# An attention step rebuilt: products with the values in one burst, scores beside transposed scores, projections at the step's end

## The reference

```python
# layer 0: 16 heads of 8, rotary positions, no mask
Q, K, V = rope(ln(x) @ Wq.T), rope(ctx @ Wk.T), ctx @ Wv.T
x = x + softmax(Q K^T / sqrt(8)) V @ Wo.T
x = x + relu(ln(x) @ quant(W1).T + b1) @ quant(W2).T + b2
# layer 1: 16 query heads on 4 key/value heads, causal and given mask, LayerNorm on the attention's output
q, k, v = ln(x) @ Wq.T + bq, ctx @ Wk.T + bk, ctx @ Wv.T + bv
x = x + ln(softmax(where(mask, q k^T / sqrt(8), min)) v) @ Wo.T + bo
# a mixture of 8 experts, one for each token
x = x + score * expert_of(ln(x))
```

## Time and profile before

| | |
|---|---|
| median of 3 runs | 578.75 us (578.5 to 578.78) |
| the profiled execution: its own time, which is its span | 578.6 us |
| tensor engine, matmuls | 493.0 us, 85% |
| vector engine | 399.0 us, 69% |
| scalar engine | 357.1 us, 62% |
| GpSimd | 372.8 us, 64% |

### The profile page before, as it was taken

The page is one execution under the profiler, slowest core; times in us unless marked ns, Lnnn a source line. Parts: engine busy times, 40 slices in busy tenths (PEclk is TensorE's granted clock), DMA queues, the critical chain, the costliest instruction groups (busy, mean ns, idle before and its releaser), DMA issues.

```text
span 578.6 us, 20130 instructions
## 1 busy us (share of the span) xinstructions
PE 493.0 (85%) x6238; PEld 361.9 (63%) x6239; DVE 399.0 (69%) x1248; ACT 357.1 (62%) x872; POOL 372.8 (64%) x755
## 2 busy tenths in 40 slices
PE   3587899999997799988999999999998834999993
PEld 2455666666665599976455555555554423999992
DVE  6687777777888578645578888888888762444441
ACT  4356677777766555653566776777765643666661
POOL 6868766676772367676556688888885561455552
PEclk9879999999999999999899999999999965999997
DMA  6664353534332860004433545444543114333330
GB/s 170 159 135 110 88 131 81 127 88 114 104 76 56 265 156 1 2 19 126 110 91 94 127 128 143 106 111 130 146 121 93 36 68 134 94 91 98 101 87 27
DMA packets 102161, 59.92 MB, mean 104 GB/s; under 512 B 20338, under 2 KB 98178, under 8 KB 102098
## 3 DMA queue, kind: packets, MB, share of 16 engines
q1 hardware_dynamic: 98738, 51.79, 35.5%
q0 software_dynamic: 2784, 6.82, 3.4%
q10 hardware_dynamic: 576, 0.53, 0.3%
HBM read 19.90 MB, written 8.81 MB: 50 GB/s over the span
## 4 chain that ended last, share of the span: by engine, by line
PE 47%; DVE 14%; issue 13%; SPq 8%; DMA 7%; POOL 5%; ACT 4%; ACTq 1%; DVEq 0%; POOLq 0%
DVE negmax L1448 6%; PE bank L688 6%; PE score L632 4%; PE bank L802 4%; PE scoreT L792 4%; DMA stack<-pieces 3%; PE bank L866 3%; PE bank L575 3%; PE bank L544 3%; SPq L404 3%; PE bank L703 2%; PE scoreT L854 2%; PE scoreT L661 2%; PE score L601 2%; SPq L470 2%
## 5 line engine op out<-in xcount | busy, mean ns | idle before, releaser
L1448 DVE TENSOR_REDUCE negmax<-score 128x8 f32<-128x1024 f32 x128 | 156.2, 1220 | 29.9 <-PE score L632 20.1
L975 ACT ACTIVATE P<-scoreT 128x1024 f32<-128x1024 f32 x128 | 131.0, 1024 | 40.1 <-PE scoreT L652 20.3
L688 PE MATMUL bank<-P,Vc 128*32 128x128 f32 x2048 | 82.7, 279 | 2.3 <-DVE product L1556 1.2
L632 PE MATMUL score<-stack 64*128 64x128 bf16 x1024 | 62.3, 221 | 15.6 <-DVE negmax L1448 9.5
L1337 POOL DMA_INDIRECT out<-by x39 | 40.2, 1031 | 51.3 <-issue 26.8
L632 PEld LDWEIGHTS score<-stack 64*128 64x128 bf16 x1024 | 33.6, 95 | 42.0 <-issue 23.1
L688 PEld LDWEIGHTS bank<-P,Vc 128*32 128x32 f32 x2048 | 48.6, 109 | 16.4 <-issue 4.3
L981 ACT COPY outs<-bank 128x256 f32<-128x256 f32 x64 | 23.7, 370 | 49.2 <-PE bank L688 49.2
L1199 POOL TENSOR_TENSOR pieces<-full,pieces 128x256 bf16<-128x256 f32 x63 | 42.2, 670 | 12.8 <-ACT pieces L956 12.8
L1202 POOL TENSOR_TENSOR pieces<-rest,pieces 128x256 bf16<-128x256 f32 x63 | 43.7, 693 | 4.9
L866 PE MATMUL bank<-M,bhT 128*128 x312 | 43.5, 282 | 0.3 <-ACT bhT L1102 0.3
(11 more groups left out here) (219 smaller groups left out, 1261.7 us busy)
## 6 DMA issues: line engine op xcount, KB each, us to landing
stack<-pieces SPq DMA_DIRECT2D x192, 128.0 KB, 2.5
ctxT<-in_ctxT SPq DMA_DIRECT2D x32, 128.0 KB, 2.4
XB<-expert_rows SPq DMA_DIRECT2D x39, 66.0 KB
XA<-expert_rows SPq DMA_DIRECT2D x39, 64.0 KB
XR<-in_x SPq DMA_DIRECT2D x4, 512.0 KB, 4.3
stack<-blank SPq DMA_DIRECT2D x32, 64.0 KB, 2.1
stack<-negpT SPq DMA_DIRECT2D x64, 32.0 KB, 1.9
M<-in_M SPq DMA_DIRECT2D x1, 2048.0 KB, 9.8
```

What stands on the lines that cost most here:

```text
L632: mm = nc.tensor.matmul(SCORE[:, r, i * 128:(i + 1) * 128], Qs[pb][rows, h, tb * S:(tb + 1) * S], Ks[pb][rows, kv, tb * S:(tb + 1) * S], s ...
L688: mm = nc.tensor.matmul(PVOUT[VCOL * i:VCOL * (i + 1), half * 128:(half + 1) * 128], Vc[:, k % BODY, at:at + VCOL], P32[:, c, i * 128:(i + ...
L975: nc.scalar.activation(P32[:, half * 2:half * 2 + 2, :], SCORET[:], ACT.Exp, scale=SCALE).then_inc(sem("exp_done"), 1)
L1448: nc.vector.tensor_reduce(negmax[:, k % 2, :, half * HQ:(half + 1) * HQ], SCORE[:].rearrange("p r (h k) -> p r h k", h=HQ), AX.X, ALU.max, ...
```

## The change

Its core is a new order of the step on each engine. On the tensor engine:

```diff
                 def step(t, j):
                     scores(t + 2, 0, j + 2)
+                    scoresT(t, 0, j)
+                    pv(t - 1, 0, j - 1)
                     pv(t - 1, 1, j - 1)
-                    scoresT(t, 0, j)
                     max_transpose(t + 1)
                     out_transpose(t - 2)
-                    regroup(t - 1, j - 1)
-                    if L and j % 2 == 0:
-                        base_logits(j + 6)
-                    project(j, 0)
-                    project(j, 1)
+                    if j % 2 == 0:
+                        project_v(j + 4)
+                    else:
+                        xn_transposes(j + 7)
+                    scores(t + 2, 1, j + 2)
                     scoresT(t, 1, j)
-                    scores(t + 2, 1, j + 2)
-                    pv(t, 0, j)
                     out_project(t - 2)
+                    regroup(t - 1)
                     if j % 2 == 0:
-                        project_v(j + 4, t)
+                        project_k(j + 6, 0)
+                        project_k(j + 6, 1)
                     else:
-                        xn_transposes(j + 7, t)
-                    if L and j % 2 == 1:
-                        ranks(j - 5)
+                        if L:
+                            base_logits(j + 7)
+                        project_q(j + 7, 0)
+                        project_q(j + 7, 1)
+                        if L:
+                            ranks(j - 5)
```

Both halves of `P` of one batch now wait for the next step, so `P32` has six half banks in place of four, three halves in turn, and `exps` waits for the product two halves back:

```diff
-                        act.wait_ge(sem("pv_done"), count(2 * (t + T0) + half - 1))
+                        act.wait_ge(sem("pv_done"), count(2 * (t + T0) + half - 2))
```

Vector engine. Layer 0: `maxima`, `rotate`, `maxima`, `denominators`, `norm_out`, `add_out(t - 2)`. Layer 1, where it was one function for both layers:

```diff
+                def step1(t, j):
+                    if j % 2 == 1:
+                        values(j + 3)
+                        if t > B:
+                            score((t - 7) // 2)
+                    else:
+                        place_of((t - 6) // 2)
+                    maxima(t + 2, 0, j + 2)
+                    add_out(t - 3, j - 3)
+                    if j % 2 == 0:
+                        base_values(j + 6)
+                        make_mask(j + 4)
+                        mean_shift((t - 6) // 2)
+                    else:
+                        choose((t - 5) // 2)
+                    maxima(t + 2, 1, j + 2)
+                    denominators(t - 1)
+                    norm_out(t - 1)
+                    out_stats(t - 1, j - 1)
+                    tile_stats(t - 3)
+                    if j % 2 == 1:
+                        carry((t - 5) // 2)
+                        if t < B:
+                            score((t - 7) // 2)
```

Scalar engine and GpSimd:

```diff
                     else:
                         high(j + 5, 0)
-                    evac_outs(t - 1)
-                    exps(t, 0)
-                    evac_max(t + 1, j + 1)
-                    evac_out(t - 2)
-                    exps(t, 1)
...
+                    exps(t, 0, j)
+                    evac_max(t + 1, j + 1)
+                    evac_out(t - 2)
+                    evac_outs(t - 1)
+                    if j % 2 == 1:
+                        evac_xnT(j + 7)
+                    exps(t, 1, j)
...
                         if j % 2 == 0:
-                            out_rstd((t - 2) // 2)
                             add_bias(j + 4)
                         else:
                             mean_rstd((t - 5) // 2)
                         for i in scattered_at(t):
                             scatter(i)
+                        if j % 2 == 0:
+                            out_rstd((t - 2) // 2)
```

More of the change, by code:

```diff
@@ L177, in build @@
         W1e = [sb(f"W1e{i}", [128, FF])[:] for i in range(TURNS)]
-        bhT = [sb(f"bhT{i}", [128, FF])[:] for i in range(TURNS)]
+        bhT = [P32[:, QUARTERS - 1 + i, :] for i in range(TURNS)]
         XA = [sb(f"XA{i}", [128, D])[:] for i in range(TURNS)]
@@ L254, in rows_of, with p_slot @@
             return tile[s:s + 15 * STRIDE + 1:STRIDE]
+        def p_slot(L, k, half):
+            return (2 * (L * B + k % BODY) + half) % SLOTS_OF_P
         def both_pieces(b, s):
@@ L270, in run_early, with body_loop @@
                 run(step, p - (PAIRS - EARLY) - AHEAD)
-        def body_loop(eng, step, first=-AHEAD, before=None, end=B + 3):
+        def body_loop(eng, step, first=-AHEAD, before=None, end=B + 3, nb=NB):
             for t in range(first, BODY):
@@ L278, in body_loop @@
                 run(step, t)
-            with eng.Fori(1, NB) as i:
+            with eng.Fori(1, nb) as i:
                 body["i"] = i
@@ L282, in body_loop @@
                     step(i * BODY + j, j)
-            for t in range(NB * BODY, end):
+            for t in range(nb * BODY, end):
                 if before and t in before:
@@ L679, in pv @@
                         pe.wait_ge(sem("outs_ready"), count(t + T0))
+                        headed_seen(t - 1)
                         pe.wait_ge(sem("v_ready"), (pair(k) + P0) + 1)
-                        if L and k % 2 == 0:
-                            pe.wait_ge(sem("ranks_read"), count(pair(k) - 2))
                     pe.wait_ge(sem("exp_done"), 2 * (t + T0) + half + 1)
@@ L729, in out_project @@
                         pe.wait_ge(sem("outT_ready"), t + T0 + 1)
+                        if isinstance(t, int) and t + 2 in folds:
+                            folds[t + 2]()
                         mm = nc.tensor.matmul(OUTX if L else OUTP, oT[:], WO, start=True, stop=True)
@@ L872, in experts @@
                 block_loop(pe, step, -2, BLOCKS)
-            step = attention(0)
-            for t in range(-AHEAD, START):
-                run(step, t)
             def gate_turn():
@@ L1009, in normalise @@
                         act.wait_ge(sem("xn_transposed"), count(p + P0))
-                        for i in range(2):
+                        for i in tiles:
                             x = X[:, 2 * p + i, :] if isinstance(p, int) else X[:, bass.ds(p * 2 + i, 1), :].rearrange("p o d -> p (o d)")
@@ L1569, in score, with step0 @@
                         nc.vector.reciprocal(XR[:, tiles, SCORE_AT], top[:, 2, tiles]).then_inc(sem("scored"), 1)
-                def step(t, j):
-                    if L and j % 2 == 1:
-                        values(j + 3)
-                        base_values(j + 5)
-                    add_out(t - 3, j - 3)
-                    if L == 0 and isinstance(t, int) and 0 <= t <= 3:
+                def step0(t, j):
+                    if isinstance(t, int) and 0 <= t <= 3:
                         x_group(3 + t)
-                    if L and t > B and j % 2 == 1:
-                        score((t - 7) // 2)
@@ L1608, in attention @@
+                step = (step0, step1)[L]
                 return step
```

127 lines of the change are left out of this document (54 added, 73 removed).

## The result

The changed kernel takes 588.8 us (median; 584.9 to 591.1) against 578.75: 1.5% **slower**, ratio 1.015 with a 95% interval of 1.0097 to 1.0203. A ratio is the recorded one, which is not exactly the quotient of the medians.

The account below looks back on a forecast made before the run. Layer 0 nearly bound by the tensor engine, layer 1 by a ring of waits through tensor, vector and GpSimd engines. 578.6 - 15.7 + 1.5 = 564.4, with 1.6 us for full rings 566 us; range 555 to 575.

Parts of the forecast that it names:

- the sum of 564.4: Whole kernel: profiled span 578.6 us, less 15.7 for layer 0, plus 1.5 for layer 1, before 1.6 us allowance.
- Outside of the attentions I count nothing: FFN and the rest outside both attentions: folds take as long, experts' tile only changes address, so 0 us.
- the ring: Layer 1, waits between maxima's transposes through vector engine and GpSimd: 6.07 plus 6.42 us, 12.5 for two steps against 12.17.
- a switch that the new order of the masks saves: Layer 1, even step's transpose of maxima to second maxima: one matmul-kind switch fewer, making that piece 1.5 us.
- by the vector engine alone: Layer 1, even to odd transpose of maxima: vector engine's work without GpSimd's wait would take 5.8 us.
- The first 7 steps: Layer 1's steps ahead of the 21, without gate work yet: 5.75 us each against about 6.0, so -1.9 us.
- the tensor engine's sum: Layer 0: tensor-engine pieces added in the new order, 4.42 even and 4.19 odd, 8.6 us for two against 10.08.
- two full rings: Layer 0: tensor engine 8.6 and DMA ring 8.6 to 8.7 us, neither without loss, so 8.8 for two steps.
- half the gain: Layer 0's 7 steps before and 8 after the steady 17: 15 x 0.32 = 4.8 us less.
- Both layers gain: Rival, chance 0.18: the transpose of maxima costs layer 1 nothing, layer 1 gains 9 us, whole kernel 554.
- The DMA ring holds layer 0 back: Rival, chance 0.17: late transfers make layer 0 9.4 us for two steps, gain 8 us in all, 572.
- The slower rival: Chance 0.10: GpSimd's even step in layer 1 pushes the split, two steps 13.9 us, 581; decides from 13.7.

Follow-up runs that it names:

- run 2: The changed kernel with layer 0 put back to its old step, only layer 1 new: 598.1 us, 1.026 of the kernel before.
- run 4: The changed kernel with the transposed-score matmuls of layer 0's last eight steps issued twice: 591.3 us, 1.016 of the kernel before.
- run 3: The changed kernel with add_out ahead of the first maxima again in layer 1's even steps: 581.2 us, 0.998 of the kernel before.
- run 5: run 3's kernel with GpSimd's out_rstd moved behind split_max of layer 1's odd step: 580.8 us, 0.992 of the kernel before.
- run 6: The changed kernel with SP's six transfers of a pair in layer 0 issued as two and four: 581.6 us, 0.997 of the kernel before.
- run 8: The changed kernel with the edits of run 3, run 5 and run 6 together: 576.8 us, 0.986 of the kernel before.
- run 9: The changed kernel with base_values of layer 1's early steps ahead of the FFN's additions: 587.5 us, 1.012 of the kernel before.

## Why the prediction was wrong

It said 566 us, faster with a chance of 0.86; the kernel is slower, at 588.8. Against the profiled span the sum of 564.4 was 18.7 us short: 4.1 in layer 0, 6.6 in layer 1, 8.8 in the FFN's part, 0.8 too much behind it.

**The step that failed is "Outside of the attentions I count nothing"**: 0 forecast, +8.8 measured. The change also gave a new order to the early steps of layer 1 that run between the FFN's tiles. I had read the order of a steady step, not that of an early one, where little stands between two dependent pieces. That is 4.0 us (run 2, at full clock). The tensor engine is idle 6.3 us in the FFN's stretch there, for 3.4 before. New are three waits of 0.46 us of the products behind `xn_transposes` for the scalar engine's copy; one of 1.49 us of `xn_transposes` for `values`, which copies the values out of the bank they share; and one of 1.15 us of the masks of the scores for the maxima. Two of them in run 2's trace:

```profile
264.75 0.41 PE L537 MATMUL bank<-eye,xn 128*128 128x128 f32 x2 [1.49 <-DVE Vc L1510]
...
272.66 0.37 PE L613 MATMUL score<-mask,negI 64*64 64x512 bf16 x1 [1.15 <-DVE negmax L1529]
```

Waits of before went in exchange: 0.57 us of the scores, and 0.5 of `project_k` for `base_values`, which is 2.30 us now and was 2.79. The last 1.1 us are busy time; one `project_k` more falls into the stretch. No run takes the new waits away one by one. The rest of the 8.8, about 4.8, is put down to time at 1.2 GHz at 185 us (3.2, of which run 4 shows 2.5) and at 257 us (1.7), of which the prediction did not speak at all.

**Layer 1: the ring was right, the size and its head were not.** The chain of waits of the changed kernel, two steps:

```profile
383.02 0.23 PE bank L714
...
384.46 1.22 DVE negmax L1451
...
388.96 0.36 DVE XR L1493
389.32 0.24 issue
389.56 0.22 PE bank L714
...
391.35 1.23 DVE negmax L1451
...
393.62 0.19 DVE omv L1477
...
394.15 0.72 POOL orstd L1226
394.88 0.21 POOL negp L1212
...
395.62 0.24 POOL negp L1217
```

The chain runs where the prediction had it: from one MT through the maxima, the small operations and `add_out` to the next (6.54 us, forecast 6.42), and from that through maxima, statistics, `out_rstd` and the split (383.02 to 395.92 in all, so 6.36, forecast 6.07). The terms read from rows held: statistics to the end of `out_rstd` 1.06 us (1.15), split 0.98 (0.99). Off were the matmuls between MT and the second maxima in the even step (389.56 to 391.35, 1.79 for 1.5), which I had taken from the old order (1.61) less "a switch that the new order of the masks saves", a saving that the trace does not show; the same piece in the odd step (383.02 to 384.46, 1.44 for 1.3); and `add_out` to MT, 0.24 for 0.05. The waits of the stretch 313 to 442 show both halves of the ring:

```profile
POOL orstd L1224 <- DVE omv L1477: 20.0, 10, 4.2
...
DVE negmax L1451 <- PE score L642: 15.6, 22, 1.3
...
PEld bank L714 <- POOL negp L1217: 11.1, 9, 1.2
PE bank L714 <- DVE XR L1493: 10.1, 11, 1.3
```

Two steps take 12.8 us on average (forecast 12.5, before 12.17): +6.4 over 21 steps for +3.4. Runs 3 and 5 show it by removal: without the first wait 6.14 us a step, without both 5.98, against the 5.8 that "by the vector engine alone" gave for one step of the two. The first 7 steps, forecast at -1.9, came to +1.2 (43.4 us for 42.2). The clock is no excuse here: both traces have 3.4 us at half clock in them (at 284 and at 277 us), and run 2, with none, still needs 41.7. So the forecast relief did not come. The last steps, which the sum left out, add some 0.5.

**Layer 0: the mechanism right, the gain 4 us too large.** One pair of steps of the changed kernel on the tensor engine, in the timeline:

```profile
101.71 0.40 PE L642 MATMUL score<-stack 64*128 64x128 bf16 x8 [0.38 <-DMA stack<-pieces]
101.94 0.40 PE L669 MATMUL scoreT<-stack 64*128 64x128 bf16 x8
102.26 1.08 PE L691 MATMUL bank<-P,Vc 128*32 128x128 f32 x32
103.28 0.23 PE L714 MATMUL bank<-eyeb,negp 128*128 128x128 bf16 x1
...
110.63 0.40 PE L642 MATMUL score<-stack 64*128 64x128 bf16 x8 [0.32 <-DMA stack<-pieces]
```

and SP's queue ahead of its first scores:

```profile
95.04 0.54 SPq L424 DMA_DIRECT2D stack<-negpT  x1
95.75 4.02 SPq L409 DMA_DIRECT2D stack<-pieces  x6
```

Scores and transposed scores take 0.55 us together (0.55 forecast), the products 1.02 (0.95), a pair of steps 8.92 (8.8); over all 17 steps 9.06 for two, -8.6 us for -10.9. And the scores do wait for the transfers: the rows of the maxima are issued at 95.04, the six transfers until 99.77, the scores begin at 101.71. Two and four instead of six (run 6) give 8.64, the 8.6 of the tensor engine's sum. So the terms stand; too small was the loss of 0.2 us a pair that I gave to two full rings (it is 0.4), and too large "half the gain" for the 15 other steps, -3.0 for -4.8. The figure of the Trainium skill that the prediction gives for a landing (DMA: Bandwidth & Descriptors, Anatomy of one DMA) was fitted there to DMAs that GpSimd issues. The transfers here are SP's; 128 KB took 2.5 us (median).

The Trainium skill says that a change of the tiling mode drains the engine (TensorEngine Tiling (Array Packing), Key Properties). Layer 0 agrees in so far as the pieces that now stand together take less time: 1.02 us for the products, 0.57 twice before, and 0.55 for scores and transposed scores, 0.40 and 0.33 apart. No run separates a drain from other costs of a change between kinds of matmul. In layer 1 the rule did not help. I wrote that no term of that ring is the tensor engine's, but two are, the matmuls between MT and the second maxima, and they came out longer than forecast.

**The rivals.** "Both layers gain" is refuted as the change was made (layer 1 is slower), and comes true with runs 3 and 5's edits. "The DMA ring holds layer 0 back" is true of the mechanism, at 0.2 us a step (4.53 for 4.32 in run 6), half of its price. The slower rival named GpSimd's even step with 13.9 us for two; it is 12.8, under its own point of decision (13.7), and only in part at that place: `add_out` alone gives 5.3 us back (run 3), and `out_rstd` on top of it 3.2 (run 5). It would not have decided alone: layer 0's gain of 11.6 is more than layer 1's loss of 8.1. That the outcome is "slower" was named, but for another reason; the sign came from what stood at nothing.

**Open** is what the 3.9 us are between this trace and the median execution (clocks of 0.949 to 0.951 for 0.957), and what sets the later stretches at half clock: the one at 257 us has its like in runs 5, 6, 8 and 9 (249 to 259 us), and none in runs 2, 3 and 4, whose early steps have nearly the same order. No run here settles that.

## What to carry to other kernels

A step's order is used more often than in its steady loop: read its first, last and interleaved uses too, and ask at each whether what stood between two dependent pieces is still there. Where an instruction sits at the end of an in-order queue and its input comes last, everything of the next step stands behind it. Moving `out_rstd` behind the next step's urgent work brought 0.16 us a step (run 5), on top of 0.25 for the place of `add_out` (run 3). Before a wait is called a loss of a change, look whether the kernel before has it too. Take a change of two layers apart first: layer 0's half was worth 1.9%, with its queue split 2.8%, and layer 1's half cost 2.6%.

## What the runs showed of the hardware

The granted clock fell to 0.5 in the middle of a kernel whose tensor engine is busy 81% of the span. Ahead of the fall at 185.0 us it was busy 2.76 of 5 us and waited 2.21 us once; with the same wait and 3.42 of 5 us busy it did not fall (run 4). At the lower level the same eight matmuls took 3.54 us for 1.97, and the 32 products 1.86 for 1.08, so saving work on the tensor engine ahead of a wait can cost time behind it: up to 3.2 us here. SP's queue needed 4.02 us to issue six transfers of 128 KB, longer than each took to land (2.5 us); where they stand in SP's order decided when the data was there (run 6, 4.32 us a step for 4.53).
